# A mixture-of-experts stage whose result scatters are ordered by thresholds made on the chip, two in flight, with GpSimd's program written out

## The reference

```python
x = x + xattn(layernorm(x), ctx, ctx, ...)       # 8 heads of 32, causal, mLSTM form
x = x + ffn(layernorm(x), w12, w3, gate_w)

# ffn, for each token t of 4096:
scores = x @ gate_w.T                            # 8 experts
topk_scores, topk_idx = top_k(scores, 2)
probs = softmax(topk_scores)                     # two experts a token
h1, h2 = split(x @ w12[e].T)                     # 256 -> 2 x 512
y[t] = sum over the two e of probs[e] * ((silu(h1) * h2) @ w3[e].T)   # 512 -> 256
```

## Time and profile before

| what | value |
|---|---|
| median of 3 runs | 795.19 us (791.96 to 798.36) |
| span of the profiled execution | 798.1 us |
| TensorE busy | 662.9 us (83%) |
| VectorE busy | 463.9 us (58%) |
| GpSimd busy | 405.0 us (51%) |
| ScalarE busy | 316.1 us (40%) |
| chain of waits: share of `DMA out_rows<-ys,ixs` | 36% |
| adding scatters, first and last issue | 379.6 and 789.6 us, 71 of them |

### The profile page before, as it was taken

How to read it: one execution, slowest core, us unless ns; L and a number is a source line. 1 busy time by engine, 2 the same in 40 slices (tenths; PEclk the granted TensorE clock), 3 DMA queues, 4 the chain that set the end, 5 groups by cost and what they waited for, 6 DMA issues and landing times.

```text
span 798.1 us, 15053 instructions
## 1 busy us (share of the span) xinstructions
PE 662.9 (83%) x3464; PEld 486.9 (61%) x3481; DVE 463.9 (58%) x940; ACT 316.1 (40%) x704; POOL 405.0 (51%) x470
## 2 busy tenths in 40 slices
PE   3781999999999994136999999999999999999981
PEld 1330566676677663114887777777677777777760
DVE  4663477485367568992676455564555655545541
ACT  3554344353245341003555444444444444434430
POOL 2234254445335331563656666666666666566653
PEclk9996898697589695556999999999999999999995
DMA  8875655355345523401232322223223232232221
GB/s 269 283 252 168 174 146 179 116 178 173 110 133 158 173 77 107 171 7 36 41 54 40 47 47 44 50 40 47 47 42 50 42 47 47 40 47 47 41 40 21
DMA packets 70952, 76.34 MB, mean 96 GB/s; under 512 B 12366, under 2 KB 63060, under 8 KB 70932
## 3 DMA queue, kind: packets, MB, share of 16 engines
q1 hardware_dynamic: 54932, 49.86, 20.2%
q0 software_dynamic: 15712, 25.73, 17.8%
q10 hardware_dynamic: 288, 0.52, 0.2%
HBM read 53.14 MB, written 22.94 MB: 95 GB/s over the span
## 4 chain that ended last, share of the span: by engine, by line
DMA 41%; PE 30%; issue 12%; DVE 8%; POOL 3%; ACT 2%; POOLq 2%; SPq 1%; DVEq 0%; ACTq 0%
DMA out_rows<-ys,ixs 36%; PE bank L1160 8%; PE bank L1174 7%; DMA qT_scratch<-qt 3%; PE bank L1155 3%; PE bank L1157 2%; PE bank L1223 2%; POOL ixs L1076 1%; PE bank L1262 1%; PE bank L1191 1%; PE bank L1264 1%; PE bank L1263 1%; PE bank L1200 1%; DVE ohp L907 1%; DVE wabs L797 1%
## 5 line engine op out<-in xcount | busy, mean ns | idle before, releaser
L1080 POOL DMA_INDIRECT out_rows<-ys,ixs x71 | 159.5, 2246 | 72.5 <-DVE ys L959 61.8
L1262 PE MATMUL bank<-w12l,xh 128*128 x284 | 125.4, 441 | 7.0 <-issue 4.8
L959 DVE TENSOR_SCALAR ys<-bank,pc 128x256 f32<-128x256 f32 x71 | 34.4, 484 | 144.9 <-DMA out_rows<-ys,ixs 140.0
L1264 PE MATMUL bank<-w12h,xh 128*128 x284 | 113.0, 398 | 0.0
L1263 PE MATMUL bank<-w12h,xl 128*128 x284 | 112.8, 397 | 0.0
L965 DVE TENSOR_TENSOR w3l<-w,w3h 128x1024 fp32r<-128x1024 f32 x71 | 87.0, 1226 | 30.8 <-issue 29.8
L1068 POOL DMA_INDIRECT xg<-token_table,ixg x71 | 71.9, 1012 | 58.4 <-POOL ixg L1065 58.4
L1174 PEld LDWEIGHTS bank<-aug,c 128*128 128x128 f32 x512 | 78.2, 219 | 37.6 <-issue 32.8
L765 DVE SCALAR_TENSOR_TENSOR c<-bank,d 128x512 f32<-128x512 f32 x64 | 44.2, 690 | 77.0 <-PE bank L1174 69.2
L624 ACT ACTIVATE sg<-bank 128x512 f32<-128x512 f32 x71 | 42.5, 599 | 115.7 <-PE bank L1264 115.7
L1290 PE MATMUL bank<-w3l,hth 128*128 128x256 f32 x284 | 76.0, 300 | 14.0 <-issue 6.9
(11 more groups left out here) (164 smaller groups left out, 1236.5 us busy)
## 6 DMA issues: line engine op xcount, KB each, us to landing
x<-in_x SPq DMA_DIRECT2D x32, 256.0 KB, 3.0
wst<-in_w12T POOLq DMA_DIRECT2D x26, 256.0 KB, 3.6
aug<-in_ctxv SPq DMA_DIRECT2D x16, 264.0 KB, 3.0
ct<-in_ctxT SPq DMA_DIRECT2D x16, 256.0 KB, 4.5
qT_scratch<-qt SPq DMA_DIRECT2D x16, 256.0 KB, 3.8
kt<-in_ctxT SPq DMA_DIRECT2D x16, 256.0 KB
qbd<-qT_scratch SPq DMA_DIRECT2D x64, 64.0 KB
out_rows<-x SPq DMA_DIRECT2D x16, 256.0 KB, 2.2
```

What stands on the lines that cost most here:

```text
L1080: q.indirect_dma_start(out=out, out_offset=bass.IndirectOffsetOnAxis(ap=IXS[i][:, 0:1], axis=0), in_=YS[i][:], in_offset=None, compute_op= ...
L1262: mm(acc, XH[i][:, k, :], wl, start=(k == 0), stop=False)
L1264: ins = mm(acc, XH[i][:, k, :], wh, start=False, stop=(k == NK - 1))
```

## The change

- `add(j)` no longer waits for all earlier scatters. It waits for the semaphore `may_add` to reach j + 1, and `may_add` is raised by SyncE alone, in a new function `order`.
- The scatters of even and odd tiles count on semaphores of their own, `y_added[0]` and `y_added[1]`. For tile j SP reads a threshold `clear[j]` from SBUF into a register and waits until the other parity's semaphore has reached it. The threshold is 16 times the number of earlier tiles of the other parity up to j - 3, and 16 more if tile j is of another expert than tile j - 1. Tiles 1 and 2 wait for their predecessor in any case. That tile j - 2 has landed follows from the wait ahead of `YS[j % 2]`, which is kept (in terms of the new semaphore).
- VectorE makes `clear` in `tile_experts`, from the experts' numbers and a table of constants `floors`: three more instructions and a wait for two new small loads.
- Slots without a pair point to one of two blocks of 128 spare rows, by the parity of the tile (`spares`), so `out` and `token_table` have 128 rows more, and SP issues two more DMAs of zeros in `later_constants`.
- GpSimd's part of the expert stage is written out for all 71 tiles, without a loop. The copies into `IXG` and `IXS`, and the waits for them, are gone: the indirect DMAs take column j of `index` itself.
- GpSimd's order is as before: `gather(j+3)`, then `add(j-1)`.

```diff
@@ -44,7 +44,7 @@
 N = B * S
 NT = N // P
 TILES = (N * TOPK + NE * (P - 1)) // P
-ROWS = N + P
+ROWS = N + 2 * P
 ROW = E + NE
 KH = HID // P
 NX = 4
...
@@ -211,8 +213,6 @@
         W3L = [sb(f"w3l{i}", [P, KH * E], F32R, on=f) for i in range(2)]
         YS = [sb(f"ys{i}", [P, E], on=f) for i in range(2)]
         PC = [sb(f"pc{i}", [P, 1], on=f) for i in range(NX)]
-        IXG = [sb(f"ixg{i}", [P, 1], U32, on=f) for i in range(NX)]
-        IXS = [sb(f"ixs{i}", [P, 1], U32, on=f) for i in range(2)]
         f.close()
 
         def sems(*names):
...
@@ -379,8 +380,9 @@
 
 
                 sp.wait_ge(zero_rows, 1)
-                sp.dma_start(table[N:ROWS, :], zrow[:]).then_inc(zero_out, 16)
-                sp.dma_start(out[N:ROWS, :], zrow[:, 0:E]).then_inc(zero_out, 16)
+                for at in (N, N + P):
+                    sp.dma_start(table[at:at + P, :], zrow[:]).then_inc(zero_out, 16)
+                    sp.dma_start(out[at:at + P, :], zrow[:, 0:E]).then_inc(zero_out, 16)
 
             def stage1(b, x):
 
...
@@ -476,6 +478,8 @@
                 sp.wait_ge(x_out[i], 16 * (B // 2))
                 sp.wait_ge(row_out[i], 16 * (B // 2))
             sp.wait_ge(score_ready, B)
+            sp.dma_start(floor16[:], floors).then_inc(slot_consts, 16)
+            sp.dma_start(spare[:], spares).then_inc(slot_consts, 16)
             sp.wait_ge(w_lo, W2 + B)
             for e in range(NE):
                 sp.dma_start(w3[:, e], w3T[:, e * KH * E:(e + 1) * KH * E].rearrange(
...
@@ -485,6 +489,25 @@
                          pw[:].rearrange("p (t e) -> p t e", e=NE)).then_inc(probs_out, 16)
             sp.wait_ge(w3_in, 16 * NE)
             sp.wait_ge(probs_out, 16)
+
+
+            def order(j, o):
+
+                at = sp.value_load(clear[0:1, bass.ds(j, 1)], min_val=16, max_val=16 * TILES)
+                sp.wait_ge(y_added[1 - o], at)
+                sp.sem_inc(may_add, 1)
+
+            sp.wait_ge(clear_ready, 1)
+            sp.sem_inc(may_add, 1)
+            for j in range(1, 3):
+                sp.wait_ge(y_added[1 - j % 2], 16)
+                sp.sem_inc(may_add, 1)
+            order(3, 1)
+            with sp.Fori(2, TILES // 2) as it:
+                for o in range(2):
+                    order(it * 2 + o, o)
+            for j in range(TILES // 2 * 2, TILES):
+                order(j, j % 2)
 
         @block.scalar
         def _(act):
...
@@ -865,6 +888,11 @@
                                         base[:, 1:NE].unsqueeze(1).broadcast_to([P, TILES, NE - 1]), ALU.is_ge))
                 st.then(v.tensor_reduce(count[:], later[:].rearrange("p (t e) -> p t e", e=NE - 1), AX.X, ALU.add))
                 st.then(v.tensor_copy(etab[:], count[:]))
+                st.then(v.tensor_tensor(turns[:, 1:], count[:, 1:], count[:, 0:TILES - 1], ALU.not_equal))
+                st.then(v.memset(clear[:, 0:1], 16))
+                dve.wait_ge(slot_consts, 32)
+                v.scalar_tensor_tensor(clear[:, 1:], turns[:, 1:], 16.0, floor16[:, 1:],
+                                       ALU.mult, ALU.add).then_inc(clear_ready, 1)
 
             v.memset(zer[:], 0.0)
             dve.wait_ge(score_ready, B)
...
@@ -918,7 +946,7 @@
             tile_experts()
             dve.wait_ge(inverted, TOPK * NT // NI)
 
-            st.then(v.tensor_scalar(fil[:], bank[1][:, TILES:2 * TILES], 0.0, io[:, P:P + 1], ALU.is_equal, ALU.mult))
+            st.then(v.scalar_tensor_tensor(fil[:], bank[1][:, TILES:2 * TILES], 0.0, spare[:], ALU.is_equal, ALU.mult))
             st.then(v.scalar_tensor_tensor(count[:], bank[1][:, TILES:2 * TILES], float(P), fil[:], ALU.mult, ALU.add))
             st.then(v.tensor_tensor(count[:], count[:], bank[1][:, 0:TILES], ALU.add))
             v.tensor_scalar(index[:], count[:], float(-P), None, ALU.add).then_inc(tables, 1)
...
@@ -955,7 +983,7 @@
 
                     dve.wait_ge(y_psum, j)
                     dve.wait_ge(pc_ready, j)
-                    wait(dve, y_added, 16 * (j - 2))
+                    wait(dve, y_added[o], 8 * (j - 1 - o))
                     v.tensor_scalar(YS[o][:], bank[6][:, 0:E], PC[(x - 1) % NX][:, 0:1], None, ALU.mult).then_inc(ys_ready, 1)
                 if up:
 
...
@@ -1057,46 +1085,38 @@
             inversion(pool, number)
 
 
-            def gather(j, x):
-
+            def gather(j):
+
+                x = j % NX
                 wait(pool, xt_psum, j - NX + 1)
                 wait(pool, pc_ready, j - NX + 1)
-                pool.sem_inc(pool_carrier, 1)
-                q.tensor_copy(IXG[x][:], index[:, bass.ds(j, 1)]).then_inc(ixg_ready, 1)
-                pool.wait_ge(ixg_ready, j + 1)
-                pool.sem_inc(pool_carrier, 1)
                 q.indirect_dma_start(out=XG[x][:], out_offset=None, in_=table,
-                                     in_offset=bass.IndirectOffsetOnAxis(ap=IXG[x][:, 0:1], axis=0)
+                                     in_offset=bass.IndirectOffsetOnAxis(ap=index[:, j:j + 1], axis=0)
                                      ).then_inc(xg_in[x], 16)
 
-            def add(j, i):
-
-                wait(pool, y_added, 16 * j)
-                pool.sem_inc(pool_carrier, 1)
-                q.tensor_copy(IXS[i][:], index[:, bass.ds(j, 1)]).then_inc(ixs_ready, 1)
-                pool.wait_ge(ixs_ready, j + 1)
+            def add(j):
+
+                o = j % 2
                 pool.wait_ge(ys_ready, j + 1)
-                pool.sem_inc(pool_carrier, 1)
-                q.indirect_dma_start(out=out, out_offset=bass.IndirectOffsetOnAxis(ap=IXS[i][:, 0:1], axis=0),
-                                     in_=YS[i][:], in_offset=None, compute_op=ALU.add).then_inc(y_added, 16)
-
-            def expert(j, x):
-
-                if not isinstance(j, int) or j + NX - 1 < TILES:
-                    gather(j + NX - 1, (x - 1) % NX)
-                if stages(j)[2]:
-                    add(j - 1, 1 - x % 2)
+                pool.wait_ge(may_add, j + 1)
+                q.indirect_dma_start(out=out, out_offset=bass.IndirectOffsetOnAxis(ap=index[:, j:j + 1], axis=0),
+                                     in_=YS[o][:], in_offset=None, compute_op=ALU.add).then_inc(y_added[o], 16)
 
             pool.wait_ge(tables, 1)
             pool.wait_ge(probs_out, 16)
             for i in range(2):
                 pool.wait_ge(x_out[i], 16 * (B // 2))
                 pool.wait_ge(row_out[i], 16 * (B // 2))
-            pool.wait_ge(zero_out, 32)
-            for x in range(NX - 1):
-                gather(x, x)
-            expert_tiles(pool, expert)
-            pool.wait_ge(y_added, 16 * TILES)
+            pool.wait_ge(zero_out, 64)
+            for j in range(NX - 1):
+                gather(j)
+            for j in range(TILES + 1):
+                if j + NX - 1 < TILES:
+                    gather(j + NX - 1)
+                if j >= 1:
+                    add(j - 1)
+            for o in range(2):
+                pool.wait_ge(y_added[o], 16 * ((TILES + 1 - o) // 2))
 
         @block.tensor
         def _(pe):
...
@@ -1338,9 +1358,13 @@
         "maskT": np.tile(np.where(p > q, MASKED, 0.0), (1, HG)).astype(bf),
         "trib": np.concatenate([p < q, np.ones((P, P))], axis=1).astype(bf),
         "marks": marks.astype(bf),
-        "iota": np.concatenate([np.broadcast_to(q, (P, P)), N + P + p], axis=1).astype(np.float32),
+        "iota": np.broadcast_to(q, (P, P)).astype(np.float32),
         "nums": np.stack(np.broadcast_arrays(p, 1 + np.repeat(np.arange(NT), TOPK)[None, :]),
                          axis=2).reshape(P, -1).astype(np.float32),
+
+        "floors": np.broadcast_to(16 * np.maximum((np.arange(TILES) - 1) // 2, 0), (P, TILES)).astype(np.float32),
+
+        "spares": (N + P + P * (np.arange(TILES) % 2)[None, :] + p).astype(np.float32),
     }
     nc = bacc.Bacc("TRN2", target_bir_lowering=False, num_devices=1)
     arrays, args = {}, []
```

More of the change, by code:

```diff
@@ L77, in build @@
 def build(nc, x, ctx, ctxv, ctxT, gkq, gkk, gkv, ibias, fbias, onw, w12T, w3T, gateT, ident, identb,
-          maskT, trib, marks, iota, nums, out):
+          maskT, trib, marks, iota, nums, floors, spares, out):
     qT_dram = nc.dram_tensor("qT_scratch", (B, P, NG, S), F32).ap()
@@ L107, in build @@
         tri = sb("tri", [P, 2, P], BF16)
-        io = sb("io", [P, P + 1])
+        io = sb("io", [P, P])
         numbers = sb("numbers", [P, 2 * TOPK * NT])
@@ L112, in build @@
         etab = sb("etab", [P, TILES], I32)
+        clear = sb("clear", [P, TILES], I32)
         index = sb("index", [P, TILES], U32)
@@ L199, in build @@
         OHN = [rt(f"ohn{i}", NI * 2 * TILES, BF16) for i in range(4)]
-        fil, count = rt("fil", TILES), rt("count", TILES)
+        fil, count, turns = rt("fil", TILES), rt("count", TILES), rt("turns", TILES)
+        floor16, spare = rt("floor16", TILES), rt("spare", TILES)
         later = rt("later", TILES * (NE - 1))
@@ L255, in build @@
```

(5 more changed lines are left out.)

## The result

The changed kernel takes 724.0 us (median of 4 runs, 721.62 to 726.55), the kernel before on the same chips 793.58 us (790.37 to 798.36). The ratio is 0.917, with a 95% interval from 0.910 to 0.925. The forecast was 728 us, in a range from 721 to 742.

What follows compares the result with a forecast made beforehand. Serial scatters bound the expert stage, TensorE next at 4.92 us: first `ys` 378.7 plus 344.4 for 70 tiles, less 2.0, plus the ending gave 731.0, 67.1 less than profiled; from 795.2 that made 728 us, range 721 to 742.

Steps and rivals of the forecast that it cites:

- The bound after the change: Expert stage: TensorE's own work binds next, at 4.92 us a tile.
- What takes the loop away: Expert stage: two scatters in flight take the serial loop away; new period 4.92 us a tile.
- The loop itself: Expert stage before: 1.27 us from landing to issue plus 4.6 us from issue to landing, 5.87 us a turn.
- GpSimd as the bound: Rival, expert stage: scatters issued inside `w3l` cost GpSimd 5.08 us a tile, total 739 us; chance 0.08.
- Starving for instructions: Rival, GpSimd's written-out part: instruction fetch stalls could make a tile 6.38 us, total 830; slower has chance 0.03.
- SyncE's grants: Expert stage: waits for SyncE's permission to scatter cost 0; without the cover of 3.8 us, 7 us.
- Two more DMAs of zeros: SP's queue ahead of the load of sequence 4: everything behind late by 0.95 us, between 0 and 2.0.
- The first gather: Start of the expert stage: gather comes without a copy, gain 0.4 us, between 0 and 1.1.
- VectorE in the routing: Routing, ahead of `fil`: three more short instructions fit in idle time, cost 0, up to 0.3 us.
- The last tile: End of the expert stage: no other tile's `half_up` between its steps, gain 2.0 us, between 0 and 2.5.
- the first case: Whole kernel: TensorE binds the expert stage, total 721 to 736 us; chance 0.76.
- The signs: Profile after: `ys` every 4.9 us, TensorE over 98% busy, scatters overlapping; wrong if first 378 us move over 2 us.

Runs made afterwards that it cites:

- e1: Kernel before with GpSimd's part written out, without its copies and semaphore increments, scatters still serial; ratio 0.917 to the kernel before.
- e2: Changed kernel with GpSimd's part in the loop of before, copies and increments included, so only the scatter order is relaxed; ratio 0.930 to the kernel before.
- e5: e1 with GpSimd's semaphore increment put back ahead of both indirect DMAs; ratio 0.917 to the kernel before.
- e9: Kernel before with only VectorE's order changed: `w3l` of tile j ahead of `ys` of tile j - 1; ratio 0.944 to the kernel before.
- e7: Changed kernel with GpSimd's semaphore increment put back ahead of each indirect DMA, relaxed order, no copies; 734.0 us in one run.
- e3: Kernel before with GpSimd's part of the expert stage written out and nothing else changed; ratio 1.000 to the kernel before.
- e8: Changed kernel with SyncE's thresholds asking for the predecessor's landing for all tiles; 723.4 us in one run.
- e6: e3 without its four semaphore increments a tile, copies kept; ratio 0.906 to the kernel before.
- e10: Kernel before, written out, without GpSimd's semaphore increment ahead of the adding DMA; copies, serial order and other increments kept; ratio 0.925 to the kernel before.

## Why the prediction was right, step by step

*The bound after the change: right.* TensorE at 4.92 us a tile was read from the eight tiles that the queue of scatters had not yet reached. It was 4.91, over 71 tiles and with TensorE busy throughout.

*What takes the loop away: wrong.* The forecast put the whole gain down to two scatters in flight, and said of the copies that "they are not counted again". Each of the parts takes the loop away (e1, e2), and in the kernel as it is the scatters hardly ever overlap. The failed step is the price of the loop without copies. I kept 0.90 us to the issue and 4.6 us to land, which makes 5.5 us and leaves the relaxed order something to do. In the changed kernel they are 0.28 and 3.8 us, 4.1 us together. Both prices were read in the kernel before, where the increment (0.6 us) and the collision (0.75 us) are part of them. Either one put right is enough to bring a serial loop to TensorE's pace: e1 still has the collision (0.27 to the issue, 4.5 to land), e5 still has the increment (0.86 and 4.0). The time came out right because the next bound caps it from whichever side one comes. For the reason that the forecast gave this is luck: the number hung on TensorE's pace alone.

*The loop itself: seen, but not understood.* I noticed that a scatter inside `w3l` takes 2.35 us and used this for a rival after the change. It was the state of the kernel before. A landing releases `ys`; `w3l` starts 0.91 us later and lasts 1.23 us; the same landing leads to the next issue after 1.27 us. So a scatter nearly always fell into `w3l` (61 of 71), and the turn was 5.87 us where its parts alone make 5.1 (e9: 5.16 in the median, 5.23 in the mean). Why this costs the kernel before 0.75 us a tile and e1 and e5, which collide too, nothing, I read from the sums: its loop free of the collision, 5.1 us, is longer than TensorE's tile, so `ys` stays tied to the landing, and `w3l` with it. In e1 and e5 the loop free of it is 3.8 + 0.27 = 4.1 and 3.9 + 0.86 = 4.7 us, `ys` comes at TensorE's pace, and the scatter falls into `w3l` only as deep as 4.9 us allow. This reading is argued from the rows; no run tests it by itself.

*GpSimd as the bound:* did not come. Its premise failed, as the scatter starts 0.28 us behind `ys` and ahead of `w3l`, and e7 shows that it would not have come even with its premise: GpSimd needs 4.4 us a tile, since the gather starts 0.30 us behind the scatter and not 0.82.

*Starving for instructions:* did not come; e3 is 1.000.

*SyncE's grants:* 0, as forecast; e8 shows it for every tile in place of seven.

*The small terms.* Two more DMAs of zeros: forecast 0.95 us; 1.0 us at sequence 4, made up by the end of the stage, so 0. The first gather: forecast 0.4 us less, measured 1.06. VectorE in the routing: 0, right. The last tile: forecast 2.0 us less; it is 4.90 - 3.84 = 1.06 us. From the last `ys` to its scatter 0.28 in place of 0.90. Sum of these against the forecast: -0.95 - 0.66 + 0.94 - 0.62 = -1.3 us.

*The profiled spans* differ by 73.3 us, the medians by 69.6, the forecast said 67.1. Of the 73.3, 3.8 us come ahead of the first gather, beyond its own 1.06, from code that was not changed. The lower edge of the first case counts up to 2 us for the end, where the term's own bound (2.5 against 2.0) leaves 0.5; nothing hangs on it.

*The signs.* The pace, the waits of `ys`, the chain of waits, TensorE's busy share and the missing copies came as the forecast listed them. Two signs did not: scatters overlap in only 3 of 71 tiles, and a landing takes 3.8 us and not about the same as before, 4.6. Both point at the failed step. And by one of its own signs the forecast would be wrong at its root, if the first 378 us move by more than 2: the first `ys` starts at 372.57 and not 378.19, 5.6 us earlier. The sign was badly chosen. In e1 and e3, whose code ahead of the experts is that of the kernel before, the first `ys` starts at 387.0 and 365.8 us.

## What to carry to other kernels

When two engines wait on the same event, look at what each does in the next microsecond: work that shares something can meet in the same place every time, and then a stall of 0.8 us a turn looks like the cost of the slow operation. Read the price of a step where it runs freely as well as where it is hit, and do the sum of a loop with each removed part alone, since two parts that are each enough don't add and the dearer one may be idle. Before building a scheme to overlap two operations, count what stands between them; here one semaphore increment per tile, a single instruction, was worth as much as the scheme.

## What the runs showed of the hardware

- A semaphore increment of GpSimd's own between its last wait and an indirect DMA delays the DMA's start by 0.6 us: 0.28 us from a copy to the DMA in e6 and e10, 0.88 us with the increment; 0.28 us from `ys` in the changed kernel, 0.87 in e7. Where the DMA follows another one and waits for nothing, the increment does not show: the gather starts 0.30 us behind the scatter in the changed kernel without it and in e7 with it.
- A subtraction of VectorE with both inputs in SBUF holds back an adding scatter that GpSimd starts inside it, for all that is left of the subtraction: the scatter then takes 1.47 us plus the rest of `w3l`. With 0.55 us left it is 2.02 (e1), with 0.81 left 2.27 (e7), with 0.87 left 2.35; over the 420 scatters of all twelve profiles that start with 0.2 to 1.2 us of `w3l` left, the sum holds within 0.04 us. A copy of one column that GpSimd starts inside `w3l` is held until it ends, too (e6, e10). The other way round there is no such effect: `w3l` takes 1.23 us with a scatter under way, in the earlier trace rows and in the changed kernel, where `w3l` starts 0.17 us behind the scatter and still takes 1.23 us. The Trainium skill, page "SBUF — State Buffer", section "Who interferes with whom", has a VectorE instruction with two SBUF inputs and a GpSimd instruction that reads SBUF block each other, by who starts first; the trace agrees with the first half and not with the second. What exactly the scatter waits for (its indices, or the writing of its descriptors) no run here tells.
- TensorE's granted clock in the mixing stage is not the same in all executions of the same code. The windows below are of the changed kernel, e1 and e3, from 140 to 210 us. At 0.83, 0.79 and 0.92, in this order, TensorE did 338, 322 and 368 matmuls in the same 70 us. The first `ys` started at 372.6, 387.0 and 365.8 us in these three profiles. So a whole span can carry 20 us that have nothing to do with the expert stage, and a stage is better compared by its own length.

```profile
140.00:210.00 70.00, 68.34 (x338) 48.62 (x342) 43.64 (x115) 29.93 (x81) 30.61 (x46) 0.83 0.51 152
```

```profile
140.00:210.00 70.00, 68.34 (x322) 48.27 (x325) 41.20 (x110) 28.78 (x77) 30.07 (x44) 0.79 0.48 144
```

```profile
140.00:210.00 70.00, 68.17 (x368) 48.78 (x372) 46.95 (x126) 33.09 (x89) 32.81 (x49) 0.92 0.52 157
```
